# A state-space layer and FP4 feed-forward on one core: small operands issued on ScalarE's queue, and the lists of the beginning laid out anew

## The reference, cut to what matters

```python
# stage 1: A [16,16], B [16,256], C [256,16], D [256,256]
xB = einsum('bsh,nh->bsn', x, B);  xD = einsum('bsh,oh->bso', x, D)
state_t = state_{t-1} @ A.T + xB_t              # scan over the 2048 steps
out = layernorm(einsum('bsn,hn->bsh', states, C) + xD) * gamma + beta
x = layernorm(x + out)
# stage 2: w_gate, w_up [704,256], w_down [256,704]
def fp4_linear(x, w):  # both quantized to FP4 values in blocks of 16, with a scale each
    return einsum('bsk,nk->bsn', fp4_quant_dequant(x), fp4_quant_dequant(w))
h = silu(fp4_linear(x, w_gate)) * fp4_linear(x, w_up)
x = layernorm(x + fp4_linear(h, w_down))
```

## Time and profile before

| what | value |
| --- | --- |
| median of 3 runs | 566.85 us (566.63 to 566.96) |
| the profiled execution | 566.68 us, span 564.9 us |
| TensorE busy | 551.6 us (98%) |
| VectorE busy | 518.0 us (92%) |
| ScalarE busy | 468.3 us (83%) |
| GpSimd busy | 494.4 us (88%) |

### The profile page before, as it was taken

The page is one execution under the profiler, slowest core; times in us unless marked ns, Lnnn a source line. Parts: engine busy times, 40 slices in busy tenths (PEclk is TensorE's granted clock), DMA queues, the critical chain, the costliest instruction groups (busy, mean ns, idle before and its releaser), DMA issues.

```text
span 564.9 us, 12830 instructions
## 1 busy us (share of the span) xinstructions
PE 551.6 (98%) x3751; PEld 495.0 (88%) x3751; DVE 518.0 (92%) x1241; ACT 468.3 (83%) x1415; POOL 494.4 (88%) x674
## 2 busy tenths in 40 slices
PE   9899999999999999999999999999999999999995
PEld 7577779999999999999999999999999999999894
DVE  4896799999999999999999999999999999999973
ACT  3557867889888998988889898888989888898756
POOL 2566887999999999999999999999999999998653
PEclk9999999999999999999999999999999999999999
...
GB/s 291 383 182 30 5 24 24 22 41 47 56 61 60 52 60 58 49 50 59 59 52 56 58 50 50 59 59 55 54 59 49 50 59 59 56 22 19 20 20 46
DMA packets 35772, 36.25 MB, mean 64 GB/s; under 512 B 6752, under 2 KB 34464, under 8 KB 34720
## 3 DMA queue, kind: packets, MB, share of 16 engines
...
## 4 chain that ended last, share of the span: by engine, by line
PE 90%; DVE 5%; ACT 2%; issue 1%; POOL 0%; POOLq 0%; DVEq 0%; ACTq 0%
PE gu L1434 41%; PE turned L1434 18%; PE yb L1434 8%; PE turned L1517 7%; PE turned L1460 2%; PE yb L1448 1%; PE grid L1293 1%; PE turned L1541 1%; PE turned L1540 1%; PE gu L1345 1%; PE yb L1345 1%; DVE scratch L1095 1%; DVE scratch L1133 1%; PE gu L1381 1%; PE turned L1381 1%
## 5 line engine op out<-in xcount | busy, mean ns | idle before, releaser
L1434 PE MATMUL gu<-wguHi,xtHi 128*128 128x512 f32 (+1 forms) x384 | 151.3, 394 | 0.4 <-DVE xtLo L1088 0.4
L1434 PE MATMUL gu<-wguLo,xtHi 128*128 128x512 f32 (+1 forms) x384 | 143.7, 374 | 0.0
L1434 PE MATMUL gu<-wguHi,xtLo 128*128 128x512 f32 (+1 forms) x384 | 143.7, 374 | 0.0
L560 POOL TENSOR_TENSOR scratch<-scratch 128x704 f32<-128x704 f32 x63 | 90.7, 1439 | 3.2 <-DVE scratch L1109 2.6
L571 POOL TENSOR_TENSOR scratch<-scratch 128x640 f32<-128x640 f32 x64 | 81.4, 1271 | 7.6 <-DVE scratch L1133 7.4
L1434 PE MATMUL turned<-wdHi,htHi 128*128 128x256 f32 x295 | 83.7, 284 | 0.0
L1434 PE MATMUL turned<-wdHi,htLo 128*128 128x256 f32 x295 | 83.6, 283 | 0.0
L1434 PEld LDWEIGHTS gu<-wguHi,xtLo 128*128 128x128 f32 x384 | 72.2, 188 | 12.3
L1434 PE MATMUL turned<-wdLo,htHi 128*128 128x256 f32 x295 | 82.6, 280 | 0.0
L1434 PEld LDWEIGHTS gu<-wguHi,xtHi 128*128 128x128 f32 x384 | 72.2, 188 | 9.9 <-DVE xtLo L1088 1.1
L1434 PEld LDWEIGHTS gu<-wguLo,xtHi 128*128 128x128 f32 x384 | 72.4, 189 | 8.2
...
## 6 DMA issues: line engine op xcount, KB each, us to landing
xT<-in_L_attn_x_dram SPq DMA_DIRECT2D x8, 1024.0 KB, 9.9
...
stTile<-statesHi SPq DMA_DIRECT2D x128, 8.0 KB, 1.7
stTile<-statesLo SPq DMA_DIRECT2D x64, 8.0 KB, 1.7
...
```

The lines of the kernel that those rows point to most:

```text
L560: nc.gpsimd.tensor_tensor(blocks(hx[:, m % 2, :]), blocks(hx[:, m % 2, :]), each_block(hRc[:, m % 4, :], FB), ALU.mult).then_inc(s_xnh, 1)
L1434: ins = nc.tensor.matmul(to, l, r, start=(first and q == 0), stop=(last and q == len(passes) - 1))
```

## The change

The diff, cut. The transfers of D, C, A and B move from SP's queue to ScalarE's, two weight loads move ahead of a wait on SP, `d_prep` puts independent steps between dependent ones, and the hand-written lists of all engines are in another order.

```diff
-    VECTOR_COPIES = (0, 2, 7, 9, 14, 15, 17, 19, 23, 25, 28)
+    VECTOR_COPIES = (2, 3, 5, 9, 12, 15, 16, 17, 18, 19, 27, 28)
...
 def _(sp):
-            with nc.allow_non_contiguous_dma("small operands"):
-                sp.dma_start(dRaw[:, :, :], D.rearrange("(k p) d -> p k d", p=P)).then_inc(s_dc, 16)
-                sp.dma_start(cRaw[:, :, :], C.rearrange("(k p) n -> p k n", p=P)).then_inc(s_dc, 16)
-                sp.dma_start(aRaw[:, :], A).then_inc(s_small, 16)
-                sp.dma_start(bRaw[:, :], B).then_inc(s_small, 16)
             load_x(0)
...
             load_x(3)
+            sp.dma_start(wg[:, full + 1:WG_ROWS, :],
+                         w_up[P - part:FF, :].rearrange("(r p) k -> p r k", p=P)).then_inc(s_wload[2], 16)
+            sp.dma_start(wX[:, WG_ROWS * H:].rearrange("p (r k) -> p r k", k=FF),
+                         w_down.rearrange("(r p) k -> p r k", p=P)).then_inc(s_wload[3], 16)
             sp.wait_ge(s_tDiag, 1)
             sp.wait_ge(s_pwc, POWER_COPIES[LOG_C + 1])
...
-            sp.dma_start(wg[:, full + 1:WG_ROWS, :],
-                         w_up[P - part:FF, :].rearrange("(r p) k -> p r k", p=P)).then_inc(s_wload[2], 16)
-            sp.dma_start(wX[:, WG_ROWS * H:].rearrange("p (r k) -> p r k", k=FF),
-                         w_down.rearrange("(r p) k -> p r k", p=P)).then_inc(s_wload[3], 16)
...
 def _(act):
+            with nc.allow_non_contiguous_dma("small operands"):
+                nc.scalar.dma_start(dRaw[:, :, :], D.rearrange("(k p) d -> p k d", p=P)).then_inc(s_dc, 16)
+                nc.scalar.dma_start(cRaw[:, :, :], C.rearrange("(k p) n -> p k n", p=P)).then_inc(s_dc, 16)
+                nc.scalar.dma_start(aRaw[:, :], A).then_inc(s_small, 16)
+                nc.scalar.dma_start(bRaw[:, :], B).then_inc(s_small, 16)
             act.wait_ge(s_half, 1)
             nc.scalar.activation(unread[:, :], neg_half[:, :], ACT.Silu)
...
             pw_init()
             powers(0)
+            xt_copy(0)
+            t_hi(0, 0)
+            xt_copy(1)
+            t_hi(0, 1)
             powers(1)
+            xt_copy(4)
             powers(2)
+            xt_copy(6)
+            xt_copy(7)
+            w_abs(0)
             powers(3)
...
 def d_prep():     (VectorE; the steps of D and C before, one after the other, each waited for)
+                nc.vector.tensor_reduce(csum[:, 0:KH], ...).then_inc(s_dsum, 1)
+                dve.wait_ge(s_dT, 2)
+                nc.vector.tensor_reduce(csum[0:N, 4:5], cBank[0:N, 0:H], AX_X, ALU.add).then_inc(s_dsum, 1)
+                (then both scalings, dHi of both halves, cHi, dLo of both halves, cLo)
...
 def _(pe):
-            unread(12, wbanks[1], ones)
+            unread(8, wbanks[1], ones)
             pe.wait_ge(s_const, 2)
             d_and_c()
+            unread(2, wbanks[1])
             powers(0)
             unread(1, wbanks[1])
-            unread(1, wbanks[1])
+            x_transposes(0)
             powers(1)
             unread(1, wbanks[1])
-            unread(1, wbanks[1])
+            x_transposes(1)
+            x_transposes(2)
+            x_transposes(3)
+            x_transposes(4)
             powers(2)
             unread(1, wbanks[1])
+            x_transposes(5)
+            x_transposes(6)
+            x_transposes(7)
+            x_transposes(8)
+            x_transposes(9)
             powers(3)
```

More of the change, by code:

```diff
@@ L898, in _ @@
             norm2(0, 1)
-            x_hi(0, 0)
+            last_states(1)
+            w_hi(9)
             nm2(0, 2)
@@ L1226, in _ @@
             x_scale(0, 1)
+            w_lo(9)
+            x_recip(0, 1)
+            link(1, 0)
             x_lo(0, 0)
-            x_recip(0, 1)
             link(1, 1)
@@ L1586, in _ @@
             pair_sums(1)
+            x_transposes(16)
+            chunk_states(0)
+            x_transposes(17)
             w_transposes(1)
-            chunk_states(0)
-            x_transposes(16)
+            link(0, 0)
             w_transposes(2)
-            link(0, 0)
-            x_transposes(17)
-            x_transposes(18)
             unread(1, yb)
             link(0, 1)
-            w_transposes(3)
             unread(1, yb)
+            x_transposes(18)
             link(0, 2)
```

291 lines of the change are left out of this document (136 added, 155 removed).

## The result

The changed kernel takes 583.24 us (median of 6 runs, 580.6 to 584.09) against 566.74 us for the kernel before in the same series: a ratio of 1.0283, with a 95% interval of 1.0263 to 1.0302. It is slower, as forecast, but by 16.5 us and not by 5, far outside the range. The profiled execution took 580.6 us, with a span of 578.8 us; before it was 564.9. So 13.9 us of span are to be found. That execution was the fastest of the six: the 2.6 us between it and the median stand in no trace.

What follows compares the result with a forecast made beforehand. It took the start of gu0(0, 0) on TensorE to bound the kernel. Terms of 0.7 + 1.7 + 1.8 + 2.0 - 1.0 gave +5.2 us on 566.68, so 571.9 us, range 567 to 576.

Steps and rivals of the forecast that it cites:

- What bounds the kernel: TensorE is busy throughout 140 to 500 us, so a later gu0(0, 0) stays late to the end, less at most 1.4 us.
- the give-back: Between 63 and 85 us TensorE idles for 1.38 us, of which a later start can swallow 0 to 1.4.
- Term (5): Stretch from 63 to 85 us: TensorE's idle time takes up part of a later start, -1.0 us.
- What gets earlier: Kernel start: fewer unread calls and earlier x loads bring link(0, 0) about 2 us earlier, a gain of 2.0 us.
- the rule: Start loads: engines alternate packets between queues, so D and C land at 6 to 7 us; with it 572.9 us.
- When beta lands: Last of the loads: beta lands at 36.1 us, as now, with bounds of 35.5 and 37.2.
- Term (1): Last links: w_norm(3) waits for beta behind four add_beta, so link(0, 8) starts at 42.7 against 41.97, +0.7 us.
- the hold: GpSimd: four add_beta ahead of w_norm(3) wait for beta, so w_norm(3) starts at 38.9 us instead of 32.29.
- Terms (2) and (4): Behind link(0, 8): four more groups of x to come, +1.7 us; more TensorE waits through the first tiles, +2.0 us.
- Term (3): TensorE's hole before the last links: the clock falls to 1.2 GHz and doubles link(0, 8), +1.8 us, then is back.
- The rival of the late landing or the clock that stays down: D and C land late, 572.9 us, or the clock stays slow behind link(0, 8), 574 to 575; chance 0.13.

Runs made afterwards that it cites:

- e8: Changed kernel with D, C, A and B on SP's queue, add_beta behind w_norm, and the lists of before up to link(0, 0): 573.30 us.
- e6: Kernel before with all four add_beta ahead of w_norm(3) on GpSimd: 575.69 us.
- e1: Changed kernel with D, C, A and B issued on SP's queue ahead of x 0 again, all lists new: 579.32 us.
- e5: Changed kernel with SP waiting for D, C, A and B to land before it issues x 0: 582.36 us.
- e14: Kernel before with D, C, A and B on ScalarE's queue and more unread calls at the start and behind C's transposes: 569.62 us.
- e16: e8 with all four add_beta ahead of w_norm(5), w_sum(3) behind link(0, 7) on VectorE, and extra unread calls: 571.55 us.
- e2: Kernel before with only D, C, A and B moved to ScalarE's queue: 577.27 us.
- e11: Changed kernel with more calls of unread where TensorE waits: 579.51 us.
- e15: Changed kernel with SP queue, order of before from link(0, 0) on, link(0, 0) ahead of w_max(3) on VectorE, 4 more unread calls: 569.73 us.
- e10: e6 with 24 more calls of unread behind link(0, 3) on TensorE: 574.07 us.

## Why the prediction had the sign right and the size wrong

**What bounds the kernel, and the give-back.** `gu0(0, 0)` late is span late: 13.84 against 13.9 us, 6.3 against 6.4 in e8, 10.5 against 10.4 in e6. Term (5), -1.0, was wrong: measured 0.

**What gets earlier.** x 0 was issued 2.0 us earlier, as forecast, and nothing on the path behind it came earlier. The first copy of x on VectorE was forecast at 9.5 and came at 13.61, for D and C came at 8.2 and not at 4.66, and `link(0, 0)` was 4.7 us late and not 2 early. Even with the old queue, in e1, the 2 us were not won: the first copy came at 10.20 and `link(0, 0)` at 31.65, 0.2 late; the count through the lists by hand was wrong there. The larger step that failed is the last one on the rule: "The wait for beta covers most of it, and only SP's part can move, by up to 1 us". The mechanism ahead of it was right: D shares the engines with x 0 and lands late (in e5, where SP's loads wait, it lands 2.7 us after its issue on the same queue). With x on another queue D's landing went from 2.6 to 6.1 us after its issue, and C's from 2.4 to 6.8. The rule of the Trainium skill ("DMA: Bandwidth & Descriptors", section "Queues, rings and completion order"), that a DMA engine takes a packet from each queue row in turn, fits these landings. But the wait for beta covered only half: `link(0, 0)` is 4.5 us later than in e1, and `link(0, 8)` still 2.2. By the medians of e1 and the changed kernel the queue cost 3.9 us (their profiled executions lie only 0.2 apart and say less), and alone in e14 3.0, since `powers(3)`, `tMat`, x 4 to 7 and beta all hang on it. `tMat` went out at 20.36 (15.8 forecast), x 6 at 30.23 (26.4).

**When beta lands.** Taken at 36.1 with 37.2 as the upper bound; it was 41.4, and even in e1, with the old queue, 39.5. There SP reached `tMat` at 17.56 and x 6 at 27.91, 1.8 and 1.5 us later than forecast, and it took 5.05 us from x 6 to beta's issue where before had 3.47 (from 21.98 to 25.45). My sum counted data from x 6 on, and not that beta's own issue was late.

**Term (1)**, +0.7 at `link(0, 8)`: measured +6.66, and +4.4 in e1. In e1 the forecast's path is there, and its size was wrong because beta landed late. In the changed kernel it is the smaller part: `link(0, 0)` was 4.70 late already, beta held `w_norm(3)` for 2.4 us and not 6.6, and 1.96 were added up to `link(0, 8)`. So the forecast had the hold as the main wait, and here the late front was. The sign would have come from the hold alone too, as e6 shows in the old lists; that it held in the changed kernel for another reason is luck. The steps behind beta were right: `add_beta` 2.78 us (2.8), `w_norm(3)` 1.06, then `w_sum(3)`, which took 1.82 beside GpSimd where I had 1.01.

**Terms (2) and (4)**, +1.7 and +2.0, are right in their sum. From `layer(0, 0)` to `gu0(0, 0)` there are 3.5 us more, with the clock at 1.00: three groups of x more stand there (a fourth stands ahead of `layer(0, 0)`), and TensorE idles for 2.9 us where it idled for 0.5. By stretches it is 2.2 up to the second layer, -0.3 to the third, and 1.5 from there on. e16 shows the first of these waits with the queue and the hold undone. The best the experiments did with this order behind `link(0, 0)` is 571.55.

**Term (3)**, +1.8, saw the mechanism and not its size. It had one fall, over when `link(0, 8)` is. The profile has four stretches, none of them in a hole of 4 us, and the last outlasts the link by 4.5 us. The sentence "Behind it I let the clock be back" failed: in e1 the clock stays at 0.50 to 53.4, in e6 for 17 us, in e2 for 20, for the most part while TensorE works. As an estimate (e11's and e15's executions), the clock is some 7 of the 16.5 us where term (3) had 1.8. The rival of the late landing or the clock that stays down, at most 574 to 575, had 0.13: both came, which it did not add up, and both were larger than it had them.

**How the parts add.** Alone in the kernel before, the queue costs 10.1 and the hold 9.5; the lists with neither cost 9.3. Together they cost 16.5 and not 29. Part of that is plain: after a late front the hold is shorter (5.8 us of wait for beta's chain ahead of `link(0, 7)` in e1, 1.35 in the changed kernel), and a stretch at 1.2 GHz can't be slowed twice. How the 16.5 divide between waits and clock is only estimated (9 to 10 and some 7): e14 and e2 divide the queue's share (3.0 and 7.7) in the old lists, e10 the hold's there roughly, and no run has the changed kernel with the clock at 1.00 throughout. Where each fall of the clock comes from, beyond the idle time ahead of it, stays open too. No version tried beats the kernel before.
